# Transposing the 1024-key tile of probabilities by VectorE squares and copies through memory instead of by TensorE

## The reference

```python
q = apply_rotary(pos, proj(Wq, bq) * scale)
k = apply_rotary(pos, proj(Wk, bk))
sim = jnp.einsum('bhid,bhjd->bhij', q, k)
sim = jnp.where(causal, -jnp.finfo(sim.dtype).max, sim)
attn = jax.nn.softmax(sim, axis=-1)
out = jnp.einsum('bhij,bhjd->bhid', attn, v)
```

## Time and profile before

| what | us |
|---|---|
| device time, median of 3 runs | 1033.1 |
| lowest and highest of the runs | 1032.43, 1033.79 |
| span of the profiled execution | 1031.9 |
| busy in it: PE, DVE, ACT, POOL | 1007.4, 776.0, 677.7, 617.9 |

### The profile page before, as it was taken

The page is one execution under the profiler, slowest core; times in us unless marked ns, Lnnn a source line. Parts: engine busy times, 40 slices in busy tenths (PEclk is TensorE's granted clock), DMA queues, the critical chain, the costliest instruction groups (busy, mean ns, idle before and its releaser), DMA issues.

```text
span 1031.9 us, 20463 instructions
## 1 busy us (share of the span) xinstructions
PE 1007.4 (98%) x6318; PEld 907.1 (88%) x6318; DVE 776.0 (75%) x1667; ACT 677.7 (66%) x1447; POOL 617.9 (60%) x470
## 2 busy tenths in 40 slices
PE   7999999999999999999999999999999999998897
...
DMA packets 41987, 56.03 MB, mean 54 GB/s; under 512 B 5508, under 2 KB 25028, under 8 KB 41924
## 3 DMA queue, kind: packets, MB, share of 16 engines
...
## 4 chain that ended last, share of the span: by engine, by line
PE 91%; DVE 2%; issue 2%; ACT 1%; POOL 1%; DMA 0%; SPq 0%; POOLq 0%; ACTq 0%; DVEq 0%
PE ps_r L1395 18%; PE ps_r L1394 18%; PE ps_r L1393 17%; PE ps_t L1552 12%; PE ps_s L1393 7%; PE ps_s L1395 6%; PE ps_s L1394 6%; PE ps_s L1400 1%; PE ps_s L1403 1%; PE ps_s L1568 1%; PE ps_r L1400 1%; PE ps_r L1402 1%; PE ps_r L1492 1%; DMA wmod_a<-in_L_wmod 0%; POOL y L712 0%
## 5 line engine op out<-in xcount | busy, mean ns | idle before, releaser
L668 POOL TENSOR_TENSOR swapped<-swapped,sin_sb 128x512 f32<-128x512 f32 x124 | 164.9, 1330 | 232.2 <-DMA swapped<-straight 231.8
L913 ACT ACTIVATE pT_hi<-ps_t 128x512 fp32r<-128x512 f32 (+3 forms) x384 | 186.9, 491 | 90.7 <-PE ps_t L1552 88.5
L1222 DVE TENSOR_TENSOR pT_lo<-ps_t,pT_hi 128x512 fp32r<-128x512 f32 (+3 forms) x384 | 202.4, 550 | 54.7 <-ACT pT_hi L913 54.4
L1287 DVE CUSTOM_DVE_ANT_0 ps_s<-ps_s,mask_wide 128x128 f32<-128x128 f32 (+7 forms) x256 | 194.5, 760 | 55.1 <-PE ps_s L1395 40.7
L678 POOL TENSOR_TENSOR qk_lo<-straight,qk_hi 128x512 fp32r<-128x512 f32 x124 | 161.8, 1318 | 114.1 <-ACT qk_hi L819 114.1
L924 ACT ACTIVATE probs<-ps_s,neg_max 128x128 f32<-128x128 f32 (+7 forms) x256 | 190.0, 742 | 34.9 <-DVE neg_max L1287 31.8
L1552 PE MATMUL ps_t<-ident,probs 128*128 128x128 f32 x1152 | 185.4, 274 | 4.9 <-DVE pT_lo L1222 2.5
L669 POOL TENSOR_TENSOR straight<-straight,cos_sb 128x512 f32<-128x512 f32 x124 | 182.6, 1472 | 0.0
L1143 DVE TENSOR_TENSOR straight<-straight,swapped 128x512 f32<-128x512 f32 x126 | 130.7, 1038 | 27.7 <-POOL straight L669 27.3
L1552 PEld LDWEIGHTS ps_t<-ident,probs 128*128 128x128 f32 x1152 | 136.9, 140 | 9.6 <-issue 5.0
L1393 PE MATMUL ps_s<-qk_hi 128*128 128x512 f32 (+4 forms) x384 | 140.4, 366 | 0.3 <-ACT probs L924 0.2
...
## 6 DMA issues: line engine op xcount, KB each, us to landing
...
x_in<-in_L_attn_x SPq DMA_DIRECT2D x4, 512.0 KB, 5.2
w_raw<-in_L_attn_Wk SPq DMA_DIRECT2D x8, 256.0 KB, 2.8
w_raw<-in_L_attn_Wq SPq DMA_DIRECT2D x8, 256.0 KB, 3.2
w_raw<-in_L_attn_Wv SPq DMA_DIRECT2D x8, 256.0 KB, 3.3
...
wo_raw<-in_L_attn_Wo SPq DMA_DIRECT2D x8, 256.0 KB, 2.7
x<-in_L_attn_x SPq DMA_DIRECT2D x4, 512.0 KB, 4.3
```

Of the source, the lines that this page charges most:

```text
L668: pool.tensor_tensor(swapped[:, q, :], swapped[:, q, :], sin_sb[:, cs], ALU.mult)
L913: nc.scalar.activation(turned_at(ORDER[step], k0, k1)(pT_hi), ps_t[:, (T_FIRST[step] + j) % 2, 0:(k1 - k0) * P].rearrange("p (k q) -> p k ...
L1222: nc.vector.tensor_tensor(turned_at(t, k0, k1)(pT_lo), ps_t[:, (T_FIRST[step] + j) % 2, 0:(k1 - k0) * P].rearrange("p (k q) -> p k q", q=P ...
L1287: nc.vector.tensor_tensor_reduce(rows, rows, halved(t, mask_wide[:, SEQ - n_keys:SEQ]), -1.0, -MASKED, ALU.add, ALU.min, accum_out=neg_max ...
```

## The change

Tile 7 of each unit, save the last unit, is no longer transposed by PE. After `exp:1`, DVE transposes its 128 x 1024 probabilities in 32 x 32 squares, each in its own place, from `probs` to `squares` (`side:1` on DVE). SP copies `squares`, 512 KB, to scratch memory outside the core (`side_out`), waits until that has landed, and reads it back in 4 DMAs of 32 partitions each (`back:1`), so that the squares stand where a full transpose would have them. ACT makes the high part of all 8 blocks in one instruction (`side:1` on ACT), DVE the low part in one (`lower:1`), both from SBUF. `turn:1.0` and `turn:1.1` are gone from PE, ACT and DVE. The product `make:P1` of the unit waits for `lower:1` too. `exp:3` stands before `out:K1` on ACT. SP now has a string: its copies stand between the swaps of Q0 and of K1.

The diff, cut to its core (`PLANS_0`, `PLANS_30` and `UNIT_29` change in the same manner):

```diff
+SIDE = (7,)
+SIDE_STEPS = [s for s in range(NQ) if ORDER[s] in SIDE]
+def has_side(u, step):
+    return step in SIDE_STEPS and u != ALL_UNITS - 1
-T_GROUPS = [(t + 4) // 4 for t in ORDER]
+T_GROUPS = [0 if s in SIDE_STEPS else (t + 4) // 4 for s, t in enumerate(ORDER)]
...
 TENSOR_PLAN = """...
-        make:P1- scores:3 turn:1.0 make:W00- make:K1+ scores:4 turn:1.1 make:W01- turn:2.0 make:Q1+
+        make:P1- scores:3 make:W00- make:K1+ scores:4 make:W01- turn:2.0 make:Q1+
 SCALAR_PLAN = """...
-        high:P1- high:K0+ high:Q0+ turn:1.0 out:K1+ turn:1.1 split:K exp:3 turn:2.0 exp:4 out:Q1+ turn:3.0
-        split:Q exp:5 turn:3.1 turn:4.0 ...
+        high:P1- high:K0+ high:Q0+ exp:3 out:K1+ split:K turn:2.0 exp:4 out:Q1+ turn:3.0
+        split:Q side:1 exp:5 turn:3.1 turn:4.0 ...
-VECTOR_PLAN = """... max:2 turn:0.0 add:Q0+ low:P1- max:3
-        sum:W00- turn:1.0 max:4 sum:W01- turn:1.1 turn:2.0 sum:W10- max:5 turn:3.0 sum:W11- add:K1+ turn:3.1
+VECTOR_PLAN = """... max:2 side:1 turn:0.0 add:Q0+ low:P1- max:3
+        sum:W00- max:4 sum:W01- turn:2.0 sum:W10- max:5 turn:3.0 lower:1 sum:W11- add:K1+ turn:3.1
+SYNC_PLAN = """swap:K0+ swap:Q0+ side:1 back:1 swap:K1+ swap:Q1+"""
...
+        squares = at("squares", A_SIDE, [P, NQ * P], F32)
+        side_p = [at(f"side_p{n}", A_SIDE + (n + 1) * 4 * KB, [P, NQ * P], F32) for n in range(2)]
+        side_out = [nc.dram_tensor(f"side_out{t}", [P, (t + 1) * P], F32).ap() for t in SIDE]
+        def from_squares(tile, t):
+            return tile[:, 0:(t + 1) * P].rearrange("p (j k c) -> p k j c", k=t + 1, c=SQUARE)
+            def move_squares(ps, u, step):
+                sp.wait_ge(squares_ready, ps.sides(u, step, 1))
+                sp.dma_start(side_out[SIDE.index(t)], squares[:, 0:(t + 1) * P]).then_inc(side_written[t], 16)
+            def move_back(ps, u, step):
+                sp.wait_ge(side_written[t], ps.units_done(u, 16))
+                dst = side_p[SIDE_SLOT[t]][:, 0:(t + 1) * P].rearrange("p (i f) -> p i f", i=P // SQUARE)
+                src = side_out[SIDE.index(t)].rearrange("(i p) (j f) -> j p i f", p=SQUARE, j=P // SQUARE)
+                for j in range(P // SQUARE):
+                    sp.dma_start(dst[j * SQUARE:j * SQUARE + SQUARE, :, :], src[j]).then_inc(side_landed[t], 16)
+            def side_high(ps, u, step):
+                act.wait_ge(side_landed[t], ps.units_done(u, 16 * SIDE_DMAS))
+                    act.wait_ge(piece_made, ps.pieces(("pv", u - 1, 1)))
+                nc.scalar.activation(turned_at(t, 0, t + 1)(pT_hi).rearrange("p k (i c) -> p k i c", c=SQUARE), from_squares(side_p[SIDE_SLOT[t]], t)[:, t::-1, :, :], ACT.Copy)\
+                    .then_inc(side_hi_ready[t], 1)
+            def side_low(ps, u, step):
+                dve.wait_ge(side_hi_ready[t], ps.units_done(u))
+                nc.vector.tensor_tensor(turned_at(t, 0, t + 1)(pT_lo).rearrange("p k (i c) -> p k i c", c=SQUARE), from_squares(side_p[SIDE_SLOT[t]], t)[:, t::-1, :, :],
+                                   turned_at(t, 0, t + 1)(pT_hi).bitcast(F32).rearrange("p k (i c) -> p k i c", c=SQUARE),
+                                   ALU.subtract).then_inc(side_ready[t], 1)
+            def side_squares(ps, u, step):
+                dve.wait_ge(exp_ready, ps.tiles(u, step + 1))
+                nc.vector.transpose(from_squares(squares, t),
+                                    probs[:, P_AT[step] * P:(P_AT[step] + t + 1) * P]
+                                    .rearrange("p (k j c) -> p k j c", k=t + 1, c=SQUARE)).then_inc(squares_ready, 1)
...
-                    pe.wait_ge(pT_ready, ps.groups(u, step, T_GROUPS[step]))
+                    pe.wait_ge(pT_ready, ps.groups(u, step + 1))
+                    for t in SIDE if chunk == 1 and u != ALL_UNITS - 1 else ():
+                        pe.wait_ge(side_ready[t], ps.units_done(u))
```

More of the change, by code:

```diff
@@ L32 @@
 TILES = UNITS * NQ
+SQUARE = 32
 EPS = 1e-5
@@ L114 @@
     SCALAR_PLAN: """out:K0+ exp:7- turn:6.0- exp:0 out:Q0+ turn:7.0- turn:7.1- float:3 high:P0- turn:0.0 exp:1 exp:2
-        high:P1- high:K0+ high:Q0+ turn:1.0 out:K1+ turn:1.1 exp:3 turn:2.0 exp:4 out:Q1+ turn:3.0
+        high:P1- high:K0+ high:Q0+ exp:3 out:K1+ turn:2.0 exp:4 out:Q1+ side:1 turn:3.0
         exp:5 turn:3.1 out:L0 turn:4.0 out:L1 high:K1+ out:L2 turn:5.0 out:L3 exp:6 turn:5.1 out:L4 high:Q1+ out:L5""",
-    VECTOR_PLAN: """largest:0 max:0 turn:6.0- turn:7.0- turn:7.1- max:1 low:P0- add:K0+ max:2 turn:0.0 add:Q0+ largest:1
-        low:P1- max:3 sum:W00- turn:1.0 max:4 sum:W01- turn:1.1 turn:2.0 sum:W10- max:5 turn:3.0 sum:W11- add:K1+ turn:3.1
+    VECTOR_PLAN: """largest:0 max:0 turn:6.0- turn:7.0- turn:7.1- max:1 low:P0- add:K0+ max:2 side:1 turn:0.0 add:Q0+ largest:1
+        low:P1- max:3 sum:W00- max:4 sum:W01- turn:2.0 sum:W10- max:5 turn:3.0 lower:1 sum:W11- add:K1+ turn:3.1
         turn:4.0 max:6 largest:2 add:Q1+ max:7 turn:5.0 turn:5.1"""}
@@ L142 @@
 UNIT_29 = {SCALAR_PLAN: """out:K0+ exp:7- turn:6.0- exp:0 out:Q0+ turn:7.0- turn:7.1- high:P0- turn:0.0 exp:1 float:0 exp:2
-        high:P1- high:K0+ high:Q0+ turn:1.0 float:1 out:K1+ turn:1.1 exp:3 turn:2.0 exp:4 out:Q1+ float:2 turn:3.0
+        high:P1- high:K0+ high:Q0+ exp:3 float:1 out:K1+ turn:2.0 exp:4 out:Q1+ float:2 side:1 turn:3.0
         exp:5 turn:3.1 turn:4.0 high:V0 high:K1+ high:V1 turn:5.0 exp:6 turn:5.1 high:Q1+"""}
@@ L176, in unit_plan @@
                 out.append((what, v, ("gate", "KQ".index(name[0]))))
+        elif what in ("side", "back", "lower"):
+            if u < ALL_UNITS - 1:
+                out.append((what, v, (int(name),)))
         elif name[0] == "V":
@@ L242, in groups, with sides, units_done @@
     def groups(self, u, step, more=0):
-        return self.count(u * T_UNIT + T_FIRST[step] + more, UNITS * T_UNIT)
+        return self.count(u * T_UNIT + first_group(u, step) + more, UNITS * T_UNIT)
+    def sides(self, u, step, more=0):
+        return self.count(u * N_SIDE + sum(s < step for s in SIDE_STEPS) + more, UNITS * N_SIDE)
+    def units_done(self, u, each=1):
+        return self.count((u + 1) * each, UNITS * each)
 def unit_batch(u):
@@ L264, in build @@
         A_WO, A_O = A_W + 12 * KB, A_W + 16 * KB
+        A_SIDE = nc.sbuf_usable_end // 32 * 32 - base - 12 * KB
         small_at = [A_SMALL]
@@ L592, in run @@
                     n = u // UNITS + 1
-                    qk = [piece for what, _, piece in unit_plan(TENSOR_PLAN, u) if what == "make" and piece[0] == "qk"]
-                    for piece in qk:
-                        swap_halves(ps, piece)
+                    for what, _, piece in unit_plan(SYNC_PLAN, u):
+                        if what == "swap":
+                            swap_halves(ps, piece)
+                        elif what == "side":
+                            move_squares(ps, u, *piece)
+                        else:
+                            move_back(ps, u, *piece)
                     if n < PAIRS and u % UNITS == 1:
@@ L1005, in do @@
                     turn_out(ps, x, *piece)
+                elif what == "side":
+                    side_high(ps, x, *piece)
                 elif what == "split":
@@ L1333, in do @@
                     turn_low(ps, x, *piece)
+                elif what == "side":
+                    side_squares(ps, x, *piece)
+                elif what == "lower":
+                    side_low(ps, x, *piece)
                 elif what == "moments":
```

64 lines of the change are left out of this document (46 added, 18 removed).

## The result

The changed kernel takes 1060.5 us, the median of 4 runs (1058.8 to 1062.2); before, in the same series, 1032.8 us, also of 4. The ratio is 1.0277, with a 95% interval from 1.0261 to 1.0292: slower by 27.7 us. The forecast was 1050.8 us, slower: the direction was right, the time 9.7 us short.

The account below looks back on a forecast made before the run. PE, busy 98%, sets the time, with DVE's unbroken stretch deciding after the change: 1.45 us stall less 0.88 us won is 0.57 us a unit, 17.7 us over 31; 1031.9 + 17.7 = 1049.6, plus 1.2: 1050.8 us, range 1023 to 1076.

Parts of the forecast that it names:

- The gain on PE: Two groups of four transposes removed from PE in each of 31 units: 0.88 us a unit, 27.3 us in all.
- The squares: DVE's transpose of 1024 columns behind `max:2`: 1.14 us, covered by 1.77 us of room, so costing nothing.
- The copies: SP's copy out (3.6 us to landing) and four back (2.3 us), landed before ACT wants them: no cost.
- The wait for ACT ahead of `lower:1`: DVE, free at 316.62, waits until ACT's `side:1` ends at 317.0: 0.4 us a unit.
- The wait for POOL inside `lower:1`: `lower:1` on DVE reads two SBUF tensors while POOL may be busy: 0.44 us, the middle of 0.22 and 0.66.
- The stall of PE: DVE's added 1.98 us less 0.53 us free at `make:K0`: PE stands 1.45 us in each unit.
- the margin of 1.04 us: Room ahead of `make:V1`, taken off DVE's added 1.98 us to leave a wait of 0.94 us there.
- two copies go with them: Copies on DVE and ACT that vanish with PE's transposes, at places with idle time: costed at nothing.
- A: Rival: DVE's cover is longer than read and the whole 27.3 us gain comes through, 1006 us; chance 0.1.
- B: Rival: `lower:1` has 0 to 0.2 us of waits, adding under 1.41 us to DVE's stretch; 1025 to 1031 us; chance 0.18.
- E: Rival: copies land late (1082 us) or squares take twice their price (1067 us); chance 0.12.

## Why the prediction was right, and what it lacked

- **The gain on PE**, 0.88 us a unit. With the low part out of the way and both turns short, three of four units take 27.3 us against 28.15 before: 0.84 us. PE's busy time is 25.0 us less, where 27.3 was forecast. Right.
- **The squares**, 1.14 us, covered. They take 1.23 us, and alone they cost nothing (1031.8 against 1031.6 us). Right. The Trainium skill ("VectorE: DVE Perf Modes", The three transpose paths) has 311 ns for a single 128x128 in bf16, which would be 2.5 us for eight; here, in float32, eight in one instruction of 1.23 us are 154 ns each, and the measurement decides.
- **The copies**, nothing. Right (1060.3 without, 1060.5 with). Out they landed in 2.6 us, where I had taken 3.6, within the bounds; back in 2.9 us, where I had taken 2.3 and the row had 2.6 at most. Both were there some 3 us before ACT wanted them.
- **The wait for ACT ahead of `lower:1`**, 0.4 us: the row shown has 0.26 us, the mean is 10.8 us / 28 = 0.39 us. Right.
- **The wait for POOL inside `lower:1`**, 0.44 us: mis-sized. With 1.22 us where POOL is away and 1.88 us on average, it is 0.66 us, and 1.05 us in the unit shown. I had taken the middle of two waits of an addition at another place, and had not asked which product of POOL `lower:1` would meet. In the unit shown it is the first product of Q1: K1's two have ended by 322.18, before `lower:1` starts. In the fourth units it is the end of K1's second. By the Trainium skill ("SBUF — State Buffer", two separate sides) of an instruction of DVE with two inputs in SBUF and one of GpSimd that reads SBUF, the one that starts first holds the shared port for its whole length, and the other blocks fully. The trace agrees: `lower:1` takes 2.27 us where it starts 0.10 us behind the start of POOL's product of 1.28 us, 1.46 us where it starts 0.9 us behind it, and 1.22 us where it starts 1.2 us behind it (the row of POOL beside the low part at 322.52):

```profile
322.42 1.28 POOL L734 TENSOR_TENSOR swapped<-swapped,sin_sb 128x512 f32<-128x512 f32 x1 [0.25 <-DMA swapped<-straight]
```

- **The stall of PE**, 1.45 us: 1.38 us in the unit shown, but all of it at `make:V1`. I had put 0.94 us there and the rest at the next `make:K0`. The place was wrong because the wait for POOL was longer: 3.13 - 0.61 = 2.52 us go in ahead of `sum:W11`, and less the margin of 1.04 us that is 1.48 us. Behind it `add:K1` gave some back (0.96 us instead of 1.35), so that `make:K0` did not wait. That the size came out in the plain units is in part luck, and in the units where POOL's product is nearly over the stall is only 0.4 us.
- **What the sum lacked**: a term for ACT's turn of the loop. The prediction says of ACT only that "two copies go with them", at no cost, and nothing here speaks against that. But it never looked at ACT's program, which grew by 28 instructions in four units. The six units with a turn fell by 1.5 to 1.8 us each when the loop was placed, 10.2 us in all; the whole run fell by 10.3 us in the medians and by 8.3 us in the profiled spans. That is about the 9.7 us that were missing.
- **What was luck.** With ACT's loop placed the time is 1050.2 us, within 0.6 us of the forecast. Two builds of the same work lay 2.7 us apart, so the agreement is closer than can be told. And it is a sum of unlike units: 28.1 to 28.3 us with the turn, 27.9 us in three, 28.8 to 29.0 us in most, 29.5 to 31.4 us in four, where the forecast had 28.8 us in all of them.
- **The rivals.** A and B were out since DVE's stretch grew by 2.52 us in the plain units, past the 1.41 us at which B decides. B's side of the balance did show in three units of the run with ACT's loop placed: POOL's product was over, DVE's stretch grew by 1.48 us only (from 0.61 to 2.09 us), and they were 0.2 us shorter than before. E was out since the copies came in time. But the 1006 us of A are nearly what the work can give: 1011.4 us with the low part at its other place.
